# Routing tables made between experts, a stage's weights loaded one stage early, and new lags in the attention of width 64

## The reference, cut to what matters

```python
x = _layernorm(x + _L0_attn_ref(x, ...))         # spectral filter and a 24-bit code
x = _layernorm(x + _L0_xattn_ref(x, ctx, ...))   # gated attention, both directions
x = _layernorm(x + _L0_ffn_ref(x, ...))          # 8 experts, given lists of tokens
x = _layernorm(x + _L1_attn_ref(x, ...))         # 16 heads of width 16
x = _layernorm(x + _L1_xattn_ref(x, ctx, ...))   # 16 heads of width 64
x = _layernorm(x + _L1_ffn_ref(x, ...))          # 32 experts, top 8 of 32
```

```python
probs = softmax(x @ gate_weight.T); topw, topi = top_k(probs, 8)
oh = one_hot(topi.reshape(-1), E)
pos = (cumsum(oh, axis=0) * oh).sum(-1) - 1           # place in the expert's list
buf = zeros(E, 256, H).at[flat_e, pos].set(flat_x, mode='drop')
h = silu(gate) * up; eo = h @ down_proj
out = sum over the 8 of tok_out * topw
```

## Time and profile before

| | |
|---|---|
| time, median of 3 runs | 2144.26 us (2138.64 to 2145.36) |
| time of the profiled execution | 2145.24 us |
| its span, first to last instruction | 2143.9 us, so 1.3 us lie around it |
| busy: PE, DVE, ACT, POOL | 1685.2, 1222.8, 1035.0, 976.2 us |
| mean granted clock of PE | 0.905 |

### The profile page before, as it was taken

The page is one execution under the profiler, slowest core; times in us unless marked ns, Lnnn a source line. Parts: engine busy times, 40 slices in busy tenths (PEclk is TensorE's granted clock), DMA queues, the critical chain, the costliest instruction groups (busy, mean ns, idle before and its releaser), DMA issues. The chain is left out here.

```text
span 2143.9 us, 23819 instructions
## 1 busy us (share of the span) xinstructions
PE 1685.2 (79%) x7419; PEld 1232.0 (57%) x7419; DVE 1222.8 (57%) x2325; ACT 1035.0 (48%) x1979; POOL 976.2 (46%) x816
## 2 busy tenths in 40 slices
PE   5488895899935787878882888998988998669892
PEld 3376674687733565656652556665655666456661
DVE  5455554666646685959853555565565565352224
ACT  1143443555511584857772665665755666242220
POOL 0000001343323474756770565665555566138884
PEclk9789998899975798989995999999999999869996
DMA  1130001444335221313002010111111111128776
GB/s 52 49 105 1 30 20 56 148 123 127 70 86 128 70 45 51 73 40 89 21 1 96 21 41 22 30 55 26 26 38 41 31 28 45 63 62 194 184 180 160
DMA packets 96787, 146.17 MB, mean 68 GB/s; under 512 B 22711, under 2 KB 61820, under 8 KB 93830
## 3 DMA queue, kind: packets, MB, share of 16 engines
q1 hardware_dynamic: 64960, 102.68, 16.6%
q0 software_dynamic: 18432, 26.36, 6.8%
q10 hardware_dynamic: 13270, 15.60, 2.4%
HBM read 101.83 MB, written 36.41 MB: 64 GB/s over the span
## 5 line engine op out<-in xcount | busy, mean ns | idle before, releaser
L2134 POOL TENSOR_TENSOR STp_lo_use<-ST_use,STp_hi_use 128x512 fp32r<-128x512 f32 x256 | 336.7, 1327 | 104.9 <-ACT ST_use L1985 101.1
L1667 POOL TENSOR_TENSOR STp_lo<-ST,STp_hi 128x512 fp32r<-128x512 f32 x192 | 254.2, 1341 | 142.7 <-ACT ST L1435 142.0
L1981 ACT ACTIVATE STp_hi_use<-bank 128x512 fp32r<-128x512 f32 x256 | 152.9, 597 | 178.1 <-PE bank L1919 174.9
L1431 ACT ACTIVATE STp_hi<-bank 128x512 fp32r<-128x512 f32 x256 | 158.8, 620 | 83.4 <-PE bank L1369 82.8
L1556 DVE TENSOR_REDUCE nmax<-bank 128x1 f32<-128x512 f32 x256 | 168.9, 680 | 42.2 <-PE bank L1358 41.8
L1358 PE MATMUL bank<-rows_k,rows_q 65*128 65x512 f32 x256 | 126.0, 501 | 62.9 <-DVE nmax L1556 44.3
L2049 DVE TENSOR_REDUCE nmax_use<-bank 128x1 f32<-128x512 f32 x256 | 170.1, 682 | 6.9 <-PE bank L1893 4.2
L1435 ACT ACTIVATE ST<-bank 128x512 f32<-128x512 f32 x256 | 160.1, 625 | 0.0
L1985 ACT ACTIVATE ST_use<-bank 128x512 f32<-128x512 f32 x256 | 151.7, 593 | 2.2 <-POOL STp_lo_use L2134 2.2
L1893 PE MATMUL bank<-ks,qs 128*128 128x512 f32 x256 | 112.2, 440 | 25.2 <-DVE nmax_use L2049 13.2
L2140 POOL CAST q<-qs 64x512 fp32r<-64x512 f32 x64 | 40.0, 625 | 197.7 <-ACT qs L2028 195.5
(11 more groups left out here) (425 smaller groups left out, 4610.6 us busy)
## 6 DMA issues: line engine op xcount, KB each, us to landing
stage<-in_W SPq DMA_DIRECT2D x16, 1024.0 KB, 4.9
Wgu<-in_Wgu SPq DMA_DIRECT2D x32, 384.0 KB
rows_q<-hop_scratch SPq DMA_DIRECT2D x32, 256.0 KB, 4.3
ks<-ks SPq DMA_DIRECT2D x64, 128.0 KB, 2.3
rinv<-rinv_scratch SPq DMA_DIRECT2D x64, 128.0 KB, 3.0
rows_k<-hop_scratch SPq DMA_DIRECT2D x24, 256.0 KB, 5.5
hop_scratch<-qkp_hi SPq DMA_DIRECT2D x20, 256.0 KB
Wda<-in_Wdn SPq DMA_DIRECT2D x32, 128.0 KB
```

The lines of the kernel that those rows point to most:

```text
L1431: A.activation(STp[u % NHI][0], bk.ap, ACT.Exp)
L1667: G.tensor_tensor(STp[u % NHI][1], ST[u % NFULL], plain(STp[u % NHI][0]), ALU.subtract).then_inc(low["pool"].sem, low["pool"].inc(u))
L1981: A.activation(STp[u % NHI][0], bk.ap, ACT.Exp)
L2134: G.tensor_tensor(STp[u % NHI][1], ST[u % NFULL], plain(STp[u % NHI][0]), ALU.subtract).then_inc(low["pool"].sem, low["pool"].inc(u))
```

## The change

Three parts, which don't touch each other.

1. The seven weights of `gated`, its first context and its biases are loaded during `spectral`, in whose instruction streams SP, ACT and POOL now also load and split them (POOL takes DVE's low parts; two of the seven are scaled in place by ACT first). The barrier at the end of `spectral` goes, and PE's first turn in `gated` waits for the normed X of its batch.
2. In `cross_heads` there are three buffers `raw` for two; DVE's evictions stand at other steps; the inverse, its ways through DRAM and the scaling stand one to four steps later; `OUTS` has its first product at step 58 for 50 and its second at 65 for 58.
3. In `routed` the way of the table through DRAM is replaced by a transposition, a product with a constant matrix `repeat`, a multiplication by the diagonal mask and a reduction. The counting is done batch by batch. Table 0 is finished alone ahead of table 1, and tables 2 and 3 are made in the loop over experts.

```diff
+def before_gated(kit):
+    kit.until_mixture, kit.until_gated = ExitStack(), ExitStack()
+    def sb(name, shape, dt=f32):
+        return kit.sb(name, shape, dt, kit.until_gated)
+    def pair(name, shape):
+        return kit.pair(name, shape, kit.until_gated)
+    kit.stage0 = {"W1": kit.sb("stage1", [P, DC, F0], f32, kit.until_mixture), "W2": kit.sb("stage2", [P, FC0, D], f32, kit.until_mixture)}
+    kit.names2 = ("Wq_c", "Wk_s", "Wv_s", "Wq_s", "Wk_c", "Wv_c", "Wg")
+    kit.W2 = {n: pair("w_" + n, [P, 2 * DC if n == "Wg" else DC, D]) for n in kit.names2}
+    kit.stage = [sb("stage%d" % z, [P, 2 * DC, D]) for z in range(2)]
+    kit.ctxp, kit.ctxT, kit.bias0 = pair("ctxp", [P, DC, S]), sb("ctxT", [P, DC, S]), sb("bias0", [P, 7, DC])
+    kit.staged2 = [Signal(kit, "staged%d" % z, range(4), step=16) for z in range(2)]
+    kit.w_high2, kit.w_low2 = Signal(kit, "w_high", kit.names2), Signal(kit, "w_low", kit.names2)
+    kit.ctx_in, kit.ctx_high, kit.ctx_low = Signal(kit, "ctx_in", range(B), step=16), Signal(kit, "ctx_high", range(B)), Signal(kit, "ctx_low", range(B))
+    kit.bias_in = Signal(kit, "bias0_in", ["bias0"], step=16)
...
+            for n, name in enumerate(names2):
+                if n > 1:
+                    SP.wait_ge(w_low2.sem, w_low2[names2[n - 2]])
+                SP.dma_start(stage[n % 2][:, 0:2 * DC if name == "Wg" else DC, :], T[name]).then_inc(staged2[n % 2].sem, staged2[n % 2].inc(n // 2))
+            SP.dma_start(kit.ctxT, T["ctxT"][0]).then_inc(kit.ctx_in.sem, kit.ctx_in.inc(0))
+            SP.dma_start(kit.bias0, T["bias0"]).then_inc(kit.bias_in.sem, kit.bias_in.inc("bias0"))
...
+            def take_weights(name):
+
+                n = names2.index(name)
+                here = stage[n % 2][:, 0:2 * DC if name == "Wg" else DC, :]
+                A.wait_ge(staged2[n % 2].sem, staged2[n % 2][n // 2])
+                if name in ("Wq_c", "Wq_s"):
+                    A.activation(here, here, ACT.Copy, scale=D ** -0.5).then_inc(a_own.sem, a_own.inc(name))
+                    A.wait_ge(a_own.sem, a_own[name])
+                A.activation(W2[name][0], here, ACT.Copy).then_inc(w_high2.sem, w_high2.inc(name))
+
+            a_own = kit.own["act"]
+            take_weights("Wq_c")
+            take_weights("Wk_s")
...
-            for b in range(1, B):
-                take(b)
+            take_weights("Wv_s")
+            take(1)
+            take_weights("Wq_s")
+            take_weights("Wk_c")
+            take(2)
+            take_weights("Wv_c")
+            take_weights("Wg")
+            A.wait_ge(kit.ctx_in.sem, kit.ctx_in[0])
+            A.activation(kit.ctxp[0], kit.ctxT, ACT.Copy).then_inc(kit.ctx_high.sem, kit.ctx_high.inc(0))
+            take(3)
...
+            for name in names2[0:3]:
+                take_weights(name)
             for b in range(B):
+                if b == 1:
+                    for name in names2[3:5]:
+                        take_weights(name)
+                if b == 2:
+                    for name in names2[5:]:
+                        take_weights(name)
+                    G.wait_ge(kit.ctx_high.sem, kit.ctx_high[0])
+                    G.tensor_tensor(kit.ctxp[1], kit.ctxT, plain(kit.ctxp[0]), ALU.subtract).then_inc(kit.ctx_low.sem, kit.ctx_low.inc(0))
...
-        nc.all_engine_barrier()
...
+                PE.wait_ge(own.sem, own["s1 normed", k])
...
-    NHI, NFULL, FOLD = 3, 2, 16
+    NHI, NFULL, NRAW, FOLD = 3, 2, 3, 16
...
-        OUTS = ((50, 0, 0), (58, 0, 1), (STEPS + 24, 1, 0), (STEPS + 25, 1, 1))
+        OUTS = ((58, 0, 0), (STEPS + 1, 0, 1), (STEPS + 24, 1, 0), (STEPS + 25, 1, 1))
+        RAW_LAG, INVERSE_LAG, RINV_OUT_LAG, RINV_LAG, ATT_LAG = 15, 17, 19, 21, 24
...
-                for r, of, half in ((3, "q", 0), (5, "k", 0), (6, "q", 1), (6, "k", 1)):
+                for r, of, half in ((4, "q", 0), (6, "k", 0), (7, "q", 1), (7, "k", 1)):
...
-                if (s - 16) % TB == 0 and 0 <= s - 16 < END:
-                    b, h, _ = place(s - 16)
+                u = s - INVERSE_LAG
...
-                if (s - 20) % TB == 0 and 0 <= s - 20 < END:
-                    b, h, _ = place(s - 20)
+                u = s - ATT_LAG
...
+            for g in range(2):
+                find_places(g)
+                turn_places(g)
+                one_to_a_partition(g)
+
+        def find_places(g):
+            z, bk = g % 2, place_bank[g]
+            PE.wait_ge(bk.free, bk.use(("slots", g)))
+            PE.wait_ge(hot_a.sem, hot_a[g])
+            PE.wait_ge(hot_v.sem, hot_v[g])
+            for t in range(NT):
+                m = PE.matmul(bk.ap[:, 0:P], A_[z][:, t, :, :].rearrange("p e j -> p (e j)"), BV[z][:, t, :], start=t == 0, stop=t == NT - 1)
+            m.then_inc(bk.full, 1)
+
+        def turn_places(g):
+            bk = place_bank[g]
+            PE.wait_ge(bk.free, bk.use(("turned", g), takers=0))
+            PE.wait_ge(placed.sem, placed[g])
+            PE.transpose(bk.ap[0:16, P:2 * P], slots[:, g, :], ident).then_inc(bk.full, 1)
+
+        def one_to_a_partition(g):
+            bk = place_bank[g]
+            PE.wait_ge(bk.free, bk.use(("table", g)))
+            PE.wait_ge(turned.sem, turned[g])
+            if g == 0:
+                PE.wait_ge(permute_in.sem, permute_in["repeat"])
+            PE.matmul(bk.ap[:, 2 * P:3 * P], repeat, slots_t, start=True, stop=True).then_inc(bk.full, 1)
...
+            compare_low(0)
+            weigh()
+            compare_high(0)
+            agree(0)
+            take_turned(0)
+            addresses(0)
+            compare_low(1)
+            compare_high(1)
+            compare_low(2)
+            agree(1)
+            take_turned(1)
+            compare_high(2)
+            addresses(1)
...
+            V.tensor_copy(slots_t[0:16, :], bk.ap[0:16, P:2 * P]).then_inc(turned.sem, turned.inc(g))
...
+            V.tensor_tensor(spread, bk.ap[:, 2 * P:3 * P].rearrange("p (t q) -> p t q", q=8), of_row, ALU.mult).then_inc(bk.free, 1)
+            V.wait_ge(bk.free, bk.free_at["table", g])
+            V.tensor_reduce(slot_n[:, g, :], spread, AX.X, ALU.add).then_inc(own.sem, own.inc(("slot_n", g)))
...
-                if e == 1:
-                    slot_table(3)
+                if e in (0, 1):
+                    find_places(e + 2)
+                if e in (1, 2):
+                    one_to_a_partition(e + 1)
...
+                if e in (0, 1):
+                    turn_places(e + 2)
...
+                if e == 0:
+                    take_tokens(3)
...
+                if e in (1, 2):
+                    addresses(e + 1)
+                if e in (0, 1):
+                    agree(e + 2)
+                    take_turned(e + 2)
                 if e == 0:
-                    addresses(3)
+                    compare_low(3)
+                    compare_high(3)
```

More of the change, by code:

```diff
@@ L651, in act @@
         def act():
-            A.dma_start(bias0, T["bias0"]).then_inc(kit.tables_in.sem, kit.tables_in.inc("bias0"))
-            for n, name in enumerate(names):
-                A.wait_ge(staged[n % 2].sem, staged[n % 2][n // 2])
-                A.activation(W[name][0], stage[n % 2][:, 0:2 * DC if name == "Wg" else DC, :], ACT.Copy, scale=scale.get(name, 1.0)).then_inc(w_high.sem, w_high.inc(name))
             A.wait_ge(own.sem, own["bias halves"])
@@ L737, in dve @@
         def dve():
[L738 to L742 removed]
+            V.wait_ge(kit.bias_in.sem, kit.bias_in["bias0"])
             for d in range(2):
@@ L2288, in turn, with count @@
                     m.then_inc(bk.full, 1)
+            def count(b):
+                if b == 0:
+                    PE.wait_ge(bank[3].free, bank[3].use(("upto", 0)))
+                else:
+                    bank[3].use(("upto", b), counted=True)
+                here = slice(b * P, (b + 1) * P)
+                for t in range(b * TB):
+                    to_all = bass.AP(marks16.tensor, marks16.offset + t * E1, [marks16.ap[0], [0, TB], [1, E1]])
+                    PE.matmul(bank[3].ap[:, here], tri[:, 1, :], to_all, start=t == 0, stop=False)
+                PE.wait_ge(marked.sem, marked[b])
+                PE.matmul(bank[3].ap[:, here], tri[:, 0, :], marks16[:, of(b), :].rearrange("p t e -> p (t e)"), start=b == 0, stop=False)
+                for t in range(TB - 1):
+                    to_later = bass.AP(marks16.tensor, marks16.offset + (b * TB + t) * E1, [marks16.ap[0], [0, TB - 1 - t], [1, E1]])
+                    m = PE.matmul(bank[3].ap[:, b * P + (t + 1) * E1:(b + 1) * P], tri[:, 1, :], to_later, start=False, stop=t == TB - 2)
+                m.then_inc(bank[3].full, 1)
             PE.wait_ge(kit.route_in.sem, table)
@@ L2309, in pe @@
-            m.then_inc(bank[0].full, 1)
-            for g in range(4):
-                z = g % 2
-                PE.wait_ge(bank[1 + z].free, bank[1 + z].use(("slots", g)))
-                PE.wait_ge(hot_a.sem, hot_a[g])
-                PE.wait_ge(hot_v.sem, hot_v[g])
```

(5 more changed lines are left out.)

215 lines of the change are left out of this document (98 added, 117 removed).

## The result

| | before | after |
|---|---|---|
| median of 5 runs | 2144.26 us (2138.64 to 2145.60) | 2126.89 us (2118.92 to 2131.81) |
| profiled execution | 2145.24 | 2131.81 |
| its span | 2143.9 | 2130.5 |

The ratio of the runs is 0.9911, with a 95% interval of 0.9883 to 0.9938: 17 us less, where 40 were forecast. The direction was right and the time lies in the range, but the gain is less than half of the forecast one.

A forecast was written before the change was run, and what follows sets the result against it. It took weight loading to bound stage 2's start, PE width 64, and the chain to the first scatter the routing: 2145.24 −19.8 −38 +18 = 2105.4, with the median 1.0 below, given as 2104 us; range 2079 to 2136.

The forecast's parts named there:

- 19.8: Start of stage 2: with weights loaded in stage 1, gated's first product starts at 92.6 for 112.39, 19.8 us less.
- rival P: Stage 1: POOL's eight subtractions, 12.6 us, all stand in DVE's way, giving 2117 us; chance 0.04.
- it gives nothing: Start of stage 2: PE's clock gives nothing back; the first 6 us of products stay at 0.50.
- −25 −6 −11 +3 +2 −1 = −38: Width 64: sum of the terms for changed lags, 38 us less, between −20 and −52.
- −25: Width 64: transposition's wait for row maxima falls from 0.98 to 0.25, −23, plus a guessed −2 for pipeline refilling.
- −6: Width 64: of the 14.0 us that the product with Wo waits for a scaling, 6 gained; bounds −14 and 0.
- −11: Width 64: the scores' twelve waits for a row maximum, 13.2 us, go with the transposition's, having the same cause.
- +3: Width 64: given back, as the copy of k's high part comes no earlier and PE, arriving sooner, waits longer; 3 us.
- +2: Width 64: other small waits given back, 2 us.
- −1: Width 64: three raw buffers let ACT's last copy of the stage go sooner, 1 us.
- Rival R2: Width 64: the stall goes on to the next wait, leaving 8 us of 38, so 2134.4 us; chance 0.19.
- +18: Routing: first scatter at 1939.0 for 1922.83 (+16.2), second expert's result 1.9 late; 18 us more, between 14 and 21.

The follow-up runs named there:

- the part alone: The kernel before with only the named part's hunks: part 1 2126.9 us, ratio 0.993; part 2 2123.8 us, ratio 0.992.
- e4: The kernel before with only part 3, the routing's tables: 2161.0 us, ratio 1.009.
- e6: The changed kernel with the sums of tables 2 and 3 at experts 4 and 9 for 0 and 1: 2114.4 us, ratio to before 0.986.
- e7: The changed kernel with unread products on PE, 36 ahead of the last products with Wo and 24 behind: 2111.9 us, ratio to before 0.987.
- e5: The changed kernel with POOL's four additions into summed at steps 37, 41, 45, 49 for 46 to 49: 2093.2 us, ratio to before 0.980.
- e8: The changed kernel with POOL waiting for DVE's normed X before its weight subtractions in stage 1: 2122.2 us, ratio to before 0.991.
- e12: The kernel before with POOL's four additions at steps 37, 41, 45, 49 of a batch: 2134.7 us, ratio 0.994.

## Why the prediction was wrong, point by point

**Part 1** was right in its size, with some luck in the details: 19.8 forecast, 20.0 by the mixture's start (19.0 in the trace of the part alone), and 16.6 in the medians of the part alone. The last `take` came at 62.51, forecast for 62.3. The first product came at 95.95, not 92.6. Of the last norm's 3.4 us, 0.7 was there at the first norm already, 1.8 came through the rival P that I gave 0.04, for which I had 12.6 at worst, and 0.9 through the low clock. The trace agrees with the Trainium skill ("SBUF — State Buffer", "Who interferes with whom", the single rule) that DVE stands still beside POOL; the row that I had weighed it against the earlier trace rows showed the same, and I set it aside for stage 1. The 5.52 us of the scaling go beyond what the Trainium skill states there, a lock held for one instruction: this one outlasted five. It also struck an instruction that I hadn't counted, since the norm has one SBUF tile as input and not two. On the other side the clock gave some back, where I had written that it gives nothing: after, products take 0.40 us again 3 us after the first one, where before it was 6, and that is worth 1.4 us by the second direction's first product (101.53, before 119.37). Where the last 2 of the 20.0 come from isn't shown; the mixture's start spreads by 5 us over the traces that have part 1.

**Part 2 is the step that failed: "−25 −6 −11 +3 +2 −1 = −38"** measured -22 (-27 in the trace of the part alone, and -19.8 in its medians, where the low clock behind it took 7). Three of its terms were wrong.

The term for what is given back, "**+3**" and "+2", had a reason for its first part only, the copy of k, and is the largest error. In the trace after, PE waits 9.1 us more at the scores, 6.4 more for q's row and 1.7 more for POOL, 17 in all for 5. So the largest term, "**−25**", was right on the wait that goes (30.5 to 0.2, and 27.8 again with the old steps) and wrong on the time, some 15: I took a wait that vanishes for time that vanishes, and 13 came back at ACT's and SP's next late work. PE's stop of 3.03 us stands once a batch, in three of the four, where ACT splits the next context (1.06 us) ahead of its q and k, and SP's copy of k goes only after it; that this order causes the stop is read from the trace and not tested.

The term "**−6**" for the product with Wo measured nothing: the wait went from that product (14.0) to the scores (14.8), because what held up DVE, POOL's unbroken run at steps 46 to 49, had not moved. I had written that the scaling "stays as slow", and still booked 6 us.

The term "−11" was right on the wait and wrong on its cause. The twelve waits at the scores (13.2) are gone in the trace after, where the only ones left for a row maximum are the four of 3.7. But with the evictions at their old steps only 2 us of them came back, beside four of 4.0, so they had not "the same cause as the first".

In the sum PE waited 25 us less (85.2 to 60.0 between first scores and turn) and was busy 3 us longer. Rival R2 had this mechanism ("the stall goes on to the next wait"), at 8 us of gain for 22.

**Part 3** was right: "**+18**" measured +17.5 alone. Its terms: the first gather 8.3 earlier (33.7 for 42.0 in e4) for 8.8, the gap to the first scatter 46.4 for a forecast 47.7, and 1.4 behind it for 1.9. That PE stands in the tables' sums with `down(0)` queued behind them is shown by e6.

**What no step had** is 8 us at the routing's start, at the low clock, and 4 in the width-16 stage. The first is seen in five of seven kernels that have part 2 and no added products, and in none of the four traces without part 2; e7 shows that it can be had back. With so few traces it isn't shown that part 2 brings it on, and no mechanism is known: PE's two idle stretches ahead of the routing are 9.4 and 6.3 us in the trace after and in those of e5 and e8, which have quick logits. The 4 us are a spread of a stage with unchanged code, which takes 520.5 to 530.0 us over the traces; the changed kernel's eleven times go from 2119 to 2134.

## What to carry to other kernels

A wait that is removed is worth what the next late engine leaves of it: for each, write down who is late next and by how much, and book nothing for a stall whose cause hasn't moved. An engine that is told to wait also frees its buffers later: in e8 that cost as much as the wait had won. Ask of a slow elementwise instruction on VectorE what GpSimd runs at that moment; here one index in the place of GpSimd's additions was worth more than the whole change. Work that is put into a loop "for free" must stand where no queue behind it feeds the pacing engine: a table that is needed 16 experts later had no business ahead of the first one.

## What the runs showed of the hardware

VectorE stood still beside GpSimd in two ways. The scaling, a multiplication of two SBUF tiles, takes 0.69 us alone and 5.52 across an unbroken run of GpSimd's subtractions and additions of 0.7 to 1.3, so it got no turn between them; in e12, with one addition in the run, 3.3. But in the trace after 13 other scalings met two subtractions in a row and took 1.4 us, while the second subtraction took 1.7 for 1.3. There VectorE did get its turn, and GpSimd waited:

```profile
1211.05 3.00 POOL L2182 TENSOR_TENSOR STp_lo_use<-ST_use,STp_hi_use 128x512 fp32r<-128x512 f32 x2 [0.40 <-ACT ST_use L2031]
...
1211.46 1.42 DVE L2143 TENSOR_TENSOR attT<-raw,rinv 64x512 f32<-64x512 f32 x1
```

What decides between the two isn't shown. The norm (`TENSOR_SCALAR`, one SBUF tile and three small operands) was held up too, but each of its instructions for one subtraction only. Of the four in the 6.38 us, two stood for 2.43 each for 0.40, beside subtractions of 2.40, and ended 0.15 behind them:

```profile
67.44 2.43 DVE L483 TENSOR_SCALAR X<-summed,mv,rstd 128x256 f32<-128x256 f32 x1
```

```profile
69.80 2.43 DVE L483 TENSOR_SCALAR X<-summed,mv,rstd 128x256 f32<-128x256 f32 x1
```

`flip` (one SBUF tile) took 2.42 for 0.42 beside a subtraction of 2.35 in e8.

The four stops of PE of 3.7 us cost nearly as much again in clock: with them gone the stage was 28 us shorter, 14.8 of them waits. Behind each stood a stretch of 3.6 to 5.4 us with products of 0.63. The three stops of 3.0 us in the trace after had such a stretch behind them too, at a granted clock of 0.50, and kept it in e5.

At the routing's start PE was busy without a gap for 21 us at the low clock in the trace after. Busy time by stretch, after (PE, PEld, DVE, ACT, POOL, then the granted clock, DMA's share and GB/s):

```profile
1821.00:1842.00 21.00, 21.00 (x112) 21.00 (x111) 5.61 (x43) 4.78 (x8) 0.00 (x0) 0.50 0.39 125
```

The same of before, whose routing starts at 1858.10:

```profile
1858.10:1862.00 3.90, 3.88 (x19) 3.90 (x20) 0.89 (x2) 1.19 (x2) 0.00 (x0) 0.50 0.99 280
1862.00:1865.00 3.00, 3.00 (x27) 3.00 (x27) 1.48 (x9) 0.59 (x1) 0.00 (x0) 0.91 1.05 383
1865.00:1868.00 3.00, 3.00 (x30) 3.00 (x29) 2.86 (x22) 0.60 (x2) 0.00 (x0) 1.00 0.57 189
```

There it rose behind the first 3.9 us of the same work. Why it rose there, and not in 21 us in the trace after, these runs don't show.
